# A recommender tower on one core: a third accumulator, two steps moved up two blocks, another order of loads, 78-row transposes

## The reference, cut to what matters

```python
# e: (512, 39, 16), gathered from 39 tables
def _cin_layer(X0, Xi, W, b):                       # H = 128
    Wr = W.reshape(H, F0_, Fi)
    return jnp.einsum('hjk,bjd,bkd->bhd', Wr, X0, Xi) + b[None, :, None]
Xi = X0 = e
for W, b in Ws:                                     # three layers
    Xi = _cin_layer(X0, Xi, W, b)
    res.append(Xi.sum(axis=2))
h = jnp.concatenate([concatenate(res), dense_ctx], axis=1)
h = jnp.maximum(h @ W_top1 + b_top1, 0.0)
h = jnp.maximum(h @ W_top2 + b_top2, 0.0)
y = h @ W_top3
```

## Time and profile before

| | us |
|---|---|
| median of 3 runs | 654.84 (652.04 to 657.98) |
| the profiled execution | 654.38 |
| its span, first to last instruction | 652.5 |
| granted TensorE clock, share of full speed | 1.00 |
| busy: TensorE / VectorE / ScalarE / GpSimd | 617.7 / 581.6 / 558.5 / 470.9 |
| mean DMA rate | 71 GB/s |

### The profile page before, as it was taken

How to read it: one execution, slowest core, us unless ns; L and a number is a source line. 1 busy time by engine, 2 the same in 40 slices (tenths; PEclk the granted TensorE clock), 3 DMA queues, 4 the chain that set the end, 5 groups by cost and what they waited for, 6 DMA issues and landing times.

```text
span 652.5 us, 14351 instructions
## 1 busy us (share of the span) xinstructions
PE 617.7 (95%) x2595; PEld 477.3 (73%) x2595; DVE 581.6 (89%) x1233; ACT 558.5 (86%) x1767; POOL 470.9 (72%) x442
## 2 busy tenths in 40 slices
PE   0389999999999999999999999999999999999998
PEld 0146788787878787878788787878787878876673
DVE  0549999999999999999999999999999999999980
ACT  3048899999999999999899989999999999999782
POOL 6778898979797989989798979798987656420000
DMA  7533404131222314040414132231405050000200
GB/s 228 135 78 88 125 19 126 34 105 53 79 81 49 109 21 137 9 137 17 126 32 121 39 91 67 67 91 39 120 8 149 1 150 5 12 18 1 65 1 0
DMA packets 44274, 46.16 MB, mean 71 GB/s; under 512 B 20896, under 2 KB 27264, under 8 KB 44233
## 3 DMA queue, kind: packets, MB, share of 16 engines
q1 hardware_dynamic: 38482, 43.59, 23.0%
q0 software_dynamic: 5120, 1.32, 2.4%
q10 hardware_dynamic: 631, 0.74, 0.4%
HBM read 44.30 MB, written 1.31 MB: 70 GB/s over the span
## 4 chain that ended last, share of the span: by engine, by line
PE 88%; issue 4%; DVE 4%; POOL 1%; ACT 1%; DMA 1%; DVEq 0%
PE ya L528 12%; PE ya L530 12%; PE ya L529 12%; PE yd L528 9%; PE yd L530 8%; PE yd L529 8%; PE misc L511 5%; PE acc L500 4%; PE acc L499 3%; PE acc L501 3%; PE acc L504 2%; DVE chain L651 2%; POOL emb L390 1%; PE yd L611 1%; PE yd L609 1%
## 5 line engine op out<-in xcount | busy, mean ns | idle before, releaser
L779 ACT ACTIVATE prods<-ya,x0t 128x128 f32<-128x128 f32 x1472 | 452.0, 519 | 40.8 <-PE ya L530 37.8
L651 DVE SCALAR_TENSOR_TENSOR chain<-yd,x0t,chain 128x128 f32<-128x128 f32 x768 | 218.2, 343 | 4.9 <-remote 4.0
L390 POOL DMA_INDIRECT emb<-in_tables,rows x160 | 158.4, 990 | 35.4 <-issue 24.3
L528 PE MATMUL ya<-w1h,x1h 128*128 128x512 f32 (+1 forms) x384 | 166.4, 433 | 3.2 <-ACT prods L779 2.1
L437 POOL TENSOR_TENSOR prod0l<-prod,prod0h 120x512 fp32r<-120x512 f32 x98 | 127.6, 1302 | 47.8 <-ACT prod0h L788 47.2
L529 PE MATMUL ya<-w1l,x1h 128*128 128x512 f32 (+1 forms) x384 | 147.5, 384 | 0.0
L530 PE MATMUL ya<-w1h,x1l 128*128 128x512 f32 (+1 forms) x384 | 147.2, 383 | 0.0
L305 POOL TENSOR_TENSOR prod<-tiles,x0a 120x512 f32<-120x512 f32 x105 | 137.3, 1308 | 12.5 <-issue 4.2
L666 DVE TENSOR_REDUCE x2t<-prods 128x128 f32<-128x1792 f32 x64 | 129.2, 2019 | 2.4 <-issue 0.3
L666 DVE TENSOR_REDUCE prods<-prods 128x128 f32<-128x1536 f32 x64 | 111.7, 1746 | 0.1
L528 PE MATMUL yd<-w1h,x1h 128*128 128x512 f32 x256 | 102.5, 400 | 1.9 <-DVE prods L651 1.6
(11 more groups left out here) (102 smaller groups left out, 620.9 us busy)
## 6 DMA issues: line engine op xcount, KB each, us to landing
tiles<-x_rows SPq DMA_DIRECT2D x236, 78.0 KB
x0a<-x_rows SPq DMA_DIRECT2D x45, 80.0 KB
emb<-in_tables,rows POOLq DMA_INDIRECT x160
w<-in_w SPq DMA_DIRECT2D x3, 832.0 KB, 5.6
w<-in_w SPq DMA_DIRECT2D x13, 192.0 KB
tiles<-x_rows SPq DMA_DIRECT2D x32, 42.0 KB
x<-x_rows SPq DMA_DIRECT2D x16, 78.0 KB
x<-x_rows SPq DMA_DIRECT2D x16, 77.8 KB
```

The lines of the kernel that those rows point to most:

```text
L390: pool.indirect_dma_start(emb[:, c % 2, fo * D:(fo + 1) * D], None, a["tables"], bass.IndirectOffsetOnAxis(ap=rows[:, c, fo:fo + 1].bitcas ...
L528: pe.matmul(out, x1h[:, c % 2, xs], w1h[:, cols], start=True, stop=False)
L651: dve.scalar_tensor_tensor(out, product, x, run if step else b1[:, :], ALU.mult, ALU.add).then_inc(yd_used, 1)
L779: mm = act.activation(prods[:, :, slot_of(q) + i], ya[(NA * g + k) % YA][:, i * H:(i + 1) * H], ACT.Copy, scale=turned(c)[:, g * F1 + j:g ...
```

## The change

- `chain` gets a third buffer. The even running sum uses buffer 0 in the groups 0 and 2 and buffer 2 in the groups 1 and 3, so step 0 of a group waits for step 14 of the group before the last, not for step 14 of the last.
- The first layer-0 tile moves from (0,3) to (0,1), in chunks 1 to 14 (`L0_AFTER`; chunk 0 has its own list, which stays).
- The layout moves from (2,1) to (1,9), and ScalarE's two copies of it from after block 2 of group 2 to after block 0. Its wait on the bank `misc` is now for the Gram product of (1,6), two blocks back.
- x0 is loaded twice instead of three times, and turned by two transposes of 78 rows each (XB = 2).
- SyncE: the part of w2 comes right behind the tile loads of its chunk, ahead of the store; the loads of x0a stand right behind the loads of x0.

```diff
-XB = 3
+XB = 2
-L0_AFTER = ((0, 3), (0, 8), (1, 3), (1, 8), (2, 3), (2, 8), (3, 1))
+L0_AFTER = ((0, 1), (0, 8), (1, 3), (1, 8), (2, 3), (2, 8), (3, 1))
 def lay_after(prev):
-    return (2, 1)
+    return (1, 9)
-        chain = sb("chain", [P, CHAINS, H])
+        chain = sb("chain", [P, CHAINS + 1, H])
 # SyncE
-            def load_layer0(x, nxt):
+            def load_blocks(x):
                 sp.wait_ge(scratch_in, 2 * 16 * (x + 1))
                 wait_done(sp, prod0_ready, T0 * x)
                 load_x0a(sp, x)
+            def load_tiles(x):
                 for i in range(T0):
                     load_tile(sp, x, i)
-                if nxt:
-                    store_x0(x + 1)
-                    load_x0(x + 1)
+            def next_chunk(x):
+                store_x0(x)
+                load_x0(x)
+                load_blocks(x)
...
-            load_layer0(1, True)
+            load_blocks(1)
+            load_tiles(1)
+            next_chunk(2)
             sp.wait_ge(w1_split, W1_PARTS)
             for x in range(2, CHUNKS):
-                load_layer0(x, x + 1 < CHUNKS)
+                load_tiles(x)
                 if x - 2 < W2_PARTS:
                     ...
                     sp.dma_start(w2[:, part, :], a["w2"][:, part, :]).then_inc(w2_in, 16)
+                if x + 1 < CHUNKS:
+                    next_chunk(x + 1)
 # TensorE, turn_x0
-                pe.transpose(misc[:, XB * F:GROUPS * F], by_group[0:F, XB, :], const[0:F, C_ID:C_ID + F]
+                pe.transpose(misc[:, XB * F:2 * XB * F], by_group[:, XB, :], const[0:XB * F, C_ID:C_ID + XB * F]
 # TensorE, chunk
                         if lay and (g, q) == lay_after(prev):
                             pe.wait_ge(x0t_ready, c + 2)
-                            wait_done(pe, g_ready, GROUPS * c + g - 1)
+                            wait_done(pe, g_ready, GROUPS * c + g)
                             lay_out(c + 2)
...
-                            if lay and g == lay_after(prev)[0]:
+                            if lay and g == lay_after(prev)[0] + 1:
                                 pe.wait_ge(x0_ready, c + 3)
 # VectorE, multiply_add
-                    wait_done(dve, yd_used, STEPS * n + step - CHAINS + 1)
+                    wait_done(dve, yd_used, STEPS * n + step - CHAINS + 1 if step else STEPS * (n - 1) - CHAINS + 1)
-                    run = chain[:, step % CHAINS, :]
+                    run = chain[:, step % CHAINS or CHAINS * (g % 2), :]
 # ScalarE, chunk
-                        if lay and (g, q - 2) == lay_after(prev):
+                        if lay and (g, q) == (lay_after(prev)[0] + 1, 0):
                             evacuate_layout(c + 2)
```

## The result

| | before | after |
|---|---|---|
| median, 20 runs each on the same chip, us | 655.46 (652.04 to 657.98) | 659.62 (655.2 to 661.37) |
| ratio, 95% interval | | 1.0054 [1.004, 1.0067] |
| the profiled execution, us | 654.38 | 657.28 |
| its span, us | 652.5 | 655.5 |
| granted TensorE clock | 1.00 | 1.00 |

The changed kernel is slower by 0.54%, some 3.5 us, within 1% as forecast. In the profiled executions the difference is 2.9 us, and it has two parts. From the start of chunk 2 to that of chunk 15 the changed kernel takes 572.16 - 111.74 = 460.4 us, the old one 456.1: 4.4 us more (4.8 were predicted for these 13 chunks). The prologue and chunks 0 and 1 took 1.3 us less.

A forecast was written before the change was run, and what follows sets the result against it. The prediction took a loop over two engines, TensorE then VectorE, to bound the kernel at 35.1 us a chunk. Layout's place 3.0, its wait 1.8 and chunk 0 0.2 made 5.0 us on 654.38: 659.4, given as 659.5, range 650 to 663.

The forecast's parts named there:

- Two legs: Chunk period 35.1 us: TensorE from group 0, block 6's Gram product to (2,1)'s end, then VectorE to next group 0's x2t sum.
- The layout's place: Layout ahead of (2,0) delays the end of (2,1), on which VectorE sits idle: 0.23 us a chunk, 3.0 us in all.
- The wait for ScalarE's Gram copy: At (1,9) the layout waits for ScalarE's copy of (1,6)'s Gram product: 0.14 us a chunk, 1.8 us in all.
- Layer-0 tile 0: Moved to (0,1), it removes the 0.28 us stall before (0,3), which returns before (0,6)'s Gram product: 0.
- The third accumulator: VectorE's step 0 no longer waits for the last group's step 14; at most 1.8 us gained, taken as 0.
- The 78-row turns: After (2,1), beside VectorE's leg: two transposes of 78 rows take as long as those of 117 and 39: 0.
- SyncE's order: Loads of x0a come some 2 us earlier, but no load ends a stall: 0, perhaps a fraction of a microsecond in the prologue.
- The sum: 3.0 + 1.8 + 0.2 = 5.0 us added to the profiled 654.38 us: 659.4, given as a median of 659.5.
- chunk 0's own wait: In chunk 0 the layout's wait for ScalarE's Gram copy may cost 0.1 to 0.3 us; taken as 0.2 us.
- The first (the stalls simply go): VectorE's leg has slack, both stalls vanish and the layout's place costs nothing: 649.5 us, at most 647.7; chance 0.15.
- The second (the accumulator): Third buffer closes VectorE's 0.29 and 0.06 us gaps, its leg loses 0.35 us: about 654.5 us, or 655 to 657; chance 0.2.
- The third (ScalarE slides on the leg): ScalarE runs later, so the layout's wait for its Gram copy puts its lag on TensorE's leg: 663.1 us; chance 0.15.

The follow-up runs named there:

- e6: The kernel before with only the 78-row turns (two loads of x0 instead of three): ratio 0.9987 to the kernel before.
- e3: The kernel before with only the layout moved, by one block from (2,1) to (2,0): ratio 1.0049 to the kernel before.
- e4: The kernel before with only the third accumulator (third chain buffer) added: ratio 0.9979 to the kernel before.
- e11: The kernel before with only SyncE's order changed (the w2 part ahead of the store): ratio 0.9995 to the kernel before.
- e2: The kernel before with only the layout moved, from (2,1) to (1,9), with its new wait: ratio 1.0072 to the kernel before.
- e1: The kernel after with only the layout put back from (1,9) to (2,1), with its old wait: 655.14 us, ratio 0.9969 to the kernel before.
- e5: The kernel before with only layer-0 tile 0 moved from (0,3) to (0,1): ratio 1.0012 to the kernel before.
- e8: e1 with layer-0 tile 1 also moved from (0,8) to (0,6): ratio 0.9933 to the kernel before.
- e9: e8 with layer-0 tile 2 also moved from (1,3) to (1,1): 642.76 us for 649.65 of the kernel before, ratio 0.9884.

## Why the prediction was right, point by point

- **Two legs.** Right. (The later chunk of the earlier trace rows is the sixth behind the one at 288.98, not the fifth; nothing hangs on it.) The five experiments on single parts agree with it, e6 best: 0.28 us less work on TensorE outside its leg changes the period by nothing.
- **The layout's place, 0.23 us a chunk.** 0.22 by e3's leg, 0.23 by its blocks, 0.26 by its period: right.
- **The wait for ScalarE's Gram copy, 0.14 us.** 0.13: right. ScalarE's copy ended 0.07 us before the load, and the stall cost the load's lateness and the load that no longer hid behind a matmul, as at (0,3) in the earlier trace rows.
- **Layer-0 tile 0, 0.** Right: the stall went from (0,3) to (0,6).
- **The third accumulator, 0.** Its mechanism was argued wrongly in one step: "I take 0, since step 1, not step 0, holds step 3 back". e4's chunks 2 to 14 say 0.8 us, its ratio 1.4 us, of a bound of 1.8.
- **The 78-row turns, "two of 78 should take as long".** Wrong on TensorE: they take 0.30 us less. Right in the sum, as they lie outside the leg.
- **SyncE's order, 0.** Right by e11, in the loop and in sum.
- **The sum.** 13 x 0.37 = 4.8 was predicted from chunk 2 to chunk 15 and 4.4 measured. The layout alone gave 4.8 (e2), and the accumulator, taken at 0, took 0.8 back (e4). The rest of the difference, 1.3 us less before chunk 2, is more than the "fraction of a microsecond" that was allowed for, and is small against the 3.8 us by which chunk 0 differs among the six profiles of the two kernels and of e1 to e4. The 0.2 us for chunk 0's own wait can't be seen beside it: no run shows this term. That the median of 659.62 meets the 659.5 so closely is in part luck: the sum was 659.4 for the profiled execution, which took 657.28, and the slowdown came out at 3.5 us, or 2.9 between the profiled executions, for 5.0. The 0.46 us to the median would have made it 659.8, and the median of the kernel before was itself 0.6 us higher in 20 runs than in the three that were known.
- **What would show it.** Period 35.4 (predicted 35.4 to 35.5), stall at (0,6) 0.76 in the chunk shown and 0.62 in the mean (0.6 to 0.8), idle time 0.94 (0.95), the gap at the branch 0.29, the load just behind ScalarE's copy: all there. The stall before (0,3) is 0.06 and not gone.

**The rivals.** The first (the stalls simply go) falls with e5. The second (the accumulator) is right in direction, at about a fifth of its size: the 0.29 us gap doesn't close, the 0.06 us one does by the end of the sum. The third (ScalarE slides on the leg) falls with the row at 338.73: ScalarE's idle time before (1,7) is 0.42 us as before.

**A wait that nobody foresaw** is nonetheless ScalarE's, at another place. In four of the chunks 3 to 13 of the kernel after, the Gram product of (3,6) waits as well. ScalarE, the last matmul of (3,2) and the weight load at (3,6), in the chunk from 360.19 (timelines):

```profile
390.57 0.63 ACT L770 ACTIVATE x1h<-x 128x512 f32 x1 [0.19 <-ACT x L767]
392.03 1.31 ACT L787 ACTIVATE prods<-ya,x0t 128x128 f32<-128x128 f32 x4 [0.82 <-PE ya L538]
393.11 0.35 ACT L759 ACTIVATE x0t<-misc 128x156 f32 x1
...
390.19 0.40 PE L538 MATMUL ya<-w1h,x1l 128*128 128x512 f32 x1
...
393.52 0.30 PEld L519 LDWEIGHTS misc<-diag,x2t 128*128 128x128 f32 x2 [0.60 <-issue]
```

The load starts 0.06 us behind the end of ScalarE's copy of the turned x0 (393.46), which is late, as ScalarE paused 0.82 us behind its copy x1h. The block that it multiplies next, (3,2), had its last matmul at 390.19 + 0.40 = 390.59, 1.4 us before. Such a pause, 1.27 us and more from the start of x1h to the next multiply where others have 0.54, is in the kernel before too, in six of its 15 chunks; there TensorE came to (3,6) later, and did not meet it. The next chunk's block (0,6) is shorter then (some 1.4 us for 1.75), so that the sum of the legs from x2t to x2t stays at 35.4: it only makes the periods go from 35.0 to 35.9 and back. It seems to go with the chip and not with the kernel: all six profiles of the two kernels and of e1 to e4 have it, in 5 to 9 of 15 chunks, and none of the seven of e5 to e11, which ran on other chips than e1 to e4, though e11 is the kernel before but for SyncE's order. The six are also those in which chunk 0 is longer. No kernel was profiled on both kinds of chip, so this isn't shown. What makes ScalarE pause isn't in the trace, and was not tried.

## What to carry to other kernels

Where two engines hand work to each other once per round, find the two points at which one of them sits idle, and count only work between them on the engine's own leg: moving 0.23 us of transposes across such a point cost 0.7% with its wait, and removing 0.28 us outside it left the period as it was. Moving one tile's matmuls off the leg gave 0.4% (e1 to e8) and moving another's into the next stall 0.5% (e8 to e9), without leaving out any work. A stall that a move removes comes back at the next wait for the same engine, so follow it there before counting it. After each step look for the leg that is now longest (here VectorE to (1,3), then GpSimd's split): the gain stops there.

## What was not expected of the hardware

- Two transposes of 78 rows by 78 columns take less room on TensorE than one of 117 and one of 39: 0.07 + 0.08 us to the next instruction for 0.20 + 0.23, 0.30 us less in the mean of two blocks. Which of rows and columns does it can't be told from this.
- Dropping a wait of one's own engine for a step two before, together with writing to a buffer of its own, let a step of VectorE start 0.03 us sooner (e4), 0.05 us in the kernel after; no run parts the wait from the buffer. The Trainium skill (VectorE: DVE Perf Modes, The DRAIN you can't avoid) has a measurement of eight copies in a row by which a semaphore behind each costs nothing extra; the trace here shows these 0.03 to 0.05 us for another pattern.
- ScalarE's pause of 0.8 us in its stream and the stops of 4 to 6 us in chunk 0 (both above): they are in the profiles of both kernels and of e1 to e4, and in none of those of e5 to e11. They can account for part of the difference between 656.25 and 649.9 us that the kernel before took on two chips: e11, which differs from the kernel before only by SyncE's order, spends 35.91 us in chunk 0 where the kernel before spent 39.09.
